# Two-layer adaLN block on one core: the chunk recurrence reordered, its widenings split between two engines, and bf16 filler products at TensorE's waits

## The reference

```python
def attn(q, k, v):
    s = einsum('bqhd,bkhd->bhqk', q, k) / sqrt(16)
    return einsum('bhqk,bkhd->bqhd', softmax(s), v)

def step(carry, xs):                         # 32 steps, one after the other
    W_in, W_out = carry
    q_t, k_t, v_t, lr_t = xs                 # 16 tokens
    k_h = softmax(einsum('blhd,bDhd->blhD', k_t, W_in)) * lr_t[..., 1:]
    q_h = softmax(einsum('blhd,bDhd->blhD', q_t, W_in))
    qk = einsum('bqhD,bkhD->bhqk', q_h, k_h) * mask
    o_t = einsum('bqhD,bDhd->bqhd', q_h, W_out) + einsum('bhqk,bkhd->bqhd', qk, v_t)
    W_out = W_out + einsum('bnhD,bnhd->bDhd', k_h, v_t)
    for _ in range(2):
        g_out = -attn(W_in, k_t, v_t)
        g_in = -attn(W_out, v_t, k_t)
        W_in = W_in - lr_in * g_in           # lr of the chunk's first token
        W_out = W_out - lr_out * g_out
    return (W_in, W_out), o_t
```

## Time and profile before

| | |
|---|---|
| time, three runs | median 3272.44 us (3271.39 to 3279.75) |
| the profiled execution | 3277.18 us, its span 3275.4 us |
| TensorE busy over the span | 2825.2 us, 86% |
| VectorE, ScalarE, GpSimd | 53%, 46%, 28% |
| granted TensorE clock over the span | 0.826 of full speed |

### The profile page before, as it was taken

The page is one execution under the profiler, slowest core; times in us unless marked ns, Lnnn a source line. Parts: engine busy times, 40 slices in busy tenths (PEclk is TensorE's granted clock), DMA queues, the critical chain, the costliest instruction groups (busy, mean ns, idle before and its releaser), DMA issues.

```text
span 3275.4 us, 89426 instructions
## 1 busy us (share of the span) xinstructions
PE 2825.2 (86%) x33209; PEld 1802.3 (55%) x33209; DVE 1720.1 (53%) x3951; ACT 1512.3 (46%) x3677; POOL 903.8 (28%) x1029
## 2 busy tenths in 40 slices
PE   6999947887888888788869999999989999999998
PEld 4444425655665656565535646556464664655556
DVE  3888834444444444444335546465564655646455
ACT  3878743233333323233225547364463635637355
POOL 0212113433333333333311313212132221323213
PEclk8999966655655565566579999999999999999999
DMA  5555571212131221211021010111101111011110
GB/s 159 154 157 163 160 158 39 55 29 56 36 68 36 50 60 29 56 36 29 9 77 39 17 56 22 52 39 53 38 15 40 39 53 39 15 44 36 53 39 14
DMA packets 386706, 189.99 MB, mean 58 GB/s; under 512 B 271664, under 2 KB 371632, under 8 KB 386224
## 3 DMA queue, kind: packets, MB, share of 16 engines
q1 hardware_dynamic: 386256, 184.01, 22.0%
HBM read 90.10 MB, written 71.30 MB: 49 GB/s over the span
## 4 chain that ended last, share of the span: by engine, by line
PE 64%; DVE 13%; ACT 9%; issue 9%; POOL 1%; DMA 1%; SPq 1%; DVEq 0%; ACTq 0%; POOLq 0%
PE psum L948 8%; PE psum L797 6%; PE psum L793 6%; PE psum L781 5%; PE psum L788 5%; PE psum L710 5%; PE psum L1029 3%; DVE arena L1592 3%; PE psum L1063 3%; PE psum L1052 3%; PE psum L987 2%; DVE arena L1659 2%; ACT arena L1385 2%; PE psum L1081 2%; PE psum L995 2%
## 5 line engine op out<-in xcount | busy, mean ns | idle before, releaser
L1233 ACT ACTIVATE arena<-psum,scan_sb 128x128 f32<-128x128 f32 x768 | 210.8, 408 | 305.4 <-PE psum L891 198.9
L1527 POOL TENSOR_TENSOR arena<-arena 128x400 f32<-128x400 f32 x256 | 218.8, 855 | 473.5 <-DVE arena L1929 473.5
L1445 POOL TENSOR_TENSOR arena<-arena 128x512 f32<-128x512 f32 x132 | 139.8, 1059 | 722.7 <-ACT arena L1250 708.5
L1659 DVE TENSOR_TENSOR arena<-psum,scan_sb 128x512 f32<-128x512 f32 x386 | 245.8, 685 | 175.1 <-PE psum L879 102.4
L1385 ACT ACTIVATE arena<-psum,arena 128x100 f32<-128x100 f32 x1024 | 268.0, 346 | 127.6 <-DVE arena L1921 127.6
L797 PEld LDWEIGHTS psum<-arena,scan_sb 32*128 32x128 f32 x1056 | 196.3, 274 | 170.2 <-issue 170.2
L793 PE MATMUL psum<-arena,scan_sb 128*128 128x512 f32 x264 | 230.7, 971 | 24.5 <-ACT arena L1239 24.4
L788 PE MATMUL psum<-arena 128*32 128x17 f32 x10240 | 197.0, 207 | 57.1 <-DVE arena L1659 22.2
L1592 DVE SCALAR_TENSOR_TENSOR arena<-psum,taps_sb,arena 128x511 f32<-128x511 f32 (+2 forms) x288 | 213.8, 747 | 61.0 <-ACT arena L1144 54.2
L781 PE MATMUL psum<-arena 128*32 128x32 f32 (+1 forms) x8192 | 190.9, 219 | 60.7 <-DVE arena L1659 43.9
L1921 DVE TENSOR_REDUCE arena<-psum 128x4 f32<-128x400 f32 x256 | 147.2, 575 | 179.0 <-PE psum L1052 177.6
(11 more groups left out here) (215 smaller groups left out, 5099.4 us busy)
## 6 DMA issues: line engine op xcount, KB each, us to landing
arena<-arena SPq DMA_DIRECT2D x144, 128.0 KB
arena<-x SPq DMA_DIRECT2D x32, 512.0 KB, 4.1
arena<-o_d SPq DMA_DIRECT2D x18, 512.0 KB, 5.8
arena<-gate_d SPq DMA_DIRECT2D x18, 512.0 KB, 6.6
v_rows_d<-arena SPq DMA_DIRECT2D x64, 136.0 KB
k_rows_d<-arena SPq DMA_DIRECT2D x64, 136.0 KB
arena<-k_rows_d SPq DMA_DIRECT2D x128, 68.0 KB, 2.1
arena<-v_rows_d SPq DMA_DIRECT2D x128, 68.0 KB, 2.1
```

The costliest lines, as they stand in the source:

```text
L1527: pool.tensor_tensor(soft, soft, c_rec[s].unsqueeze(2).broadcast_to([P, 4, KEYS]), ALU.mult).then_inc(c_pool.mark(f"prob{s}{f}"), 1)
L1659: return dve.tensor_tensor(dst.rearrange("p (t x a) -> p t x a", x=PP, a=INNER)[:, tiles], src.rearrange("p (t a) -> p t a", a=INNER)[:, t ...
```

## The change

On TensorE, `running` is taken apart into `sums(j)` and `add_state(js)`, which adds the state for two j at once with j as the inner loop. Halves of widenings disappear: every `scores` and `updates` walks over all four strips. `p1v` and `p2v` come ahead of `khv`, and `two`, `tw1` and `b0`, `b1` stand in pairs. `keep_busy` (new) issues 19 filler products a chunk into a bank that nobody reads. The two states' `ti1` and `ti` change places. On the other engines, each of now 8 widenings is done by two engines at once: VectorE writes partitions 0 to 63 and four copies in one instruction, ScalarE partitions 64 to 127 and the four others in four instructions. What neither writes stays zero from one memset of 9216 columns ahead of the loop. In the diff the first `spread` is ScalarE's, the second VectorE's. Stages A and C, the loads and GpSimd's steps are as before, though GpSimd and ScalarE wait for `r01` or `r23` where they waited for one `r`.

```diff
+            def keep_busy(count):
+                for _ in range(count):
+                    pe.matmul(bank[5][:, 0:2 * KT * KEYS], identb[:], mask_sb[:, 0:2].rearrange("p a b -> p (a b)"), start=True, stop=True)
...
-            def running(j, w_out):
-                mm = pe.matmul(bank[6 + j % 2][:], causal, kv[:, j], start=True, stop=False, skip_group_check=True)
-                rows = slice(j * NST, (j + 1) * NST)
+            def sums(j):
+                return pe.matmul(bank[6 + j % 2][:], causal, kv[:, j], start=True, stop=False, skip_group_check=True)
+
+            def add_state(js, w_out):
                 for a in range(INNER):
-                    dst = bank[6 + j % 2][:].rearrange("q (p a d) -> q p a d", p=PP, a=INNER)[:, :, a]
-                    mm = pe.matmul(dst, pick_row[rows, a], w_out[rows].rearrange("q (p d) -> q p d", p=PP),
-                                   start=False, stop=(a == INNER - 1), skip_group_check=True)
+                    for j in js:
+                        rows = slice(j * NST, (j + 1) * NST)
+                        dst = bank[6 + j % 2][:].rearrange("q (p a d) -> q p a d", p=PP, a=INNER)[:, :, a]
+                        mm = pe.matmul(dst, pick_row[rows, a], w_out[rows].rearrange("q (p d) -> q p d", p=PP),
+                                       start=False, stop=(a == INNER - 1), skip_group_check=True)
...
+                    keep_busy(4)
+                    pe.wait_ge(dve.sem, dve.before(c, "xi"))
                     pe.wait_ge(act.sem, act.before(c, "xi"))
-                    pe.wait_ge(dve.sem, dve.before(c, "xb11"))
...
+                    pe.wait_ge(dve.sem, dve.at(c, "x1"))
+                    pe.wait_ge(act.sem, act.at(c, "x1"))
+                    updates(grid(bank[0][:, 0:PP * ROW17], ROW17), pb_1, v_rows[i % 2], every).then_inc(mine.mark("p1v"), 1)
...
             def spread(dst, src):
-                for x in range(PP):
-                    ins = act.activation(dst.rearrange("p (t x a) -> p t x a", x=PP, a=INNER)[:, :, x],
-                                         src.rearrange("p (t a) -> p t a", a=INNER), ACT.Copy, scale=mask8[:, x:x + 1])
+                for x in range(PP // 2, PP):
+                    ins = act.activation(dst.rearrange("p (t x a) -> p t x a", x=PP, a=INNER)[upper, :, x],
+                                         src.rearrange("p (t a) -> p t a", a=INNER)[upper], ACT.Copy, scale=mask8[upper, x:x + 1])
...
-            dve.memset(st_in1, 0.0).then_inc(st_dve.mark("no_st"), 1)
+            dve.memset(arena[:, 0:9 * TILES * NST], 0.0).then_inc(st_dve.mark("no_st"), 1)
...
-            def spread(dst, src, h):
-                tiles = slice(h * TILES // 2, (h + 1) * TILES // 2)
-                shape = [P, TILES // 2, PP, INNER]
+            def spread(dst, src, h=0):
+                rows, xs = slice(h * P // 2, (h + 1) * P // 2), slice(h * PP // 2, (h + 1) * PP // 2)
+                shape = [P // 2, TILES, PP // 2, INNER]
...
-                    dve.wait_ge(pe.sem, pe.at(c, "pb1"))
-                    dve.reciprocal(i_inv, i_new[:, :, :, HD]).then_inc(mine.mark("irec"), 1)
...
+                    for r, (before, after, name) in enumerate(((w_in_now, w_in_1, "wi1"), (w_in_1, w_in_now, "wi"))):
+                        dve.wait_ge(pe.sem, pe.at(c, f"pb{r}"))
+                        dve.reciprocal(i_inv[r], i_new[r][:, :, HD]).then_inc(mine.mark(f"irec{r}"), 1)
...
+                    dve.wait_ge(pe.sem, pe.at(c, "ti1"))
+                    spread(st_in1, bank[2][:, 0:P]).then_inc(mine.mark("xs"), 1)
                     dve.wait_ge(pe.sem, pe.at(c, "ti"))
-                    for h in range(2):
-                        spread(st_in2, bank[3][:, 3 * P:4 * P], h).then_inc(mine.mark(f"xi{h}"), 1)
+                    spread(st_in2, bank[1][:, 0:P]).then_inc(mine.mark("xi"), 1)
```

283 lines of the change are left out of this document (141 added, 142 removed).

## The result

The changed kernel takes 2909.8 us in the median of four runs (2907.7 to 2923.4), 0.889 of the kernel before (95% interval 0.886 to 0.892). The forecast was 2841 with a range of 2780 to 2965: the time lies in the range, 69 us above the forecast. The profiled execution has a span of 2907.3 us.

A forecast was written before the change was run, and what follows sets the result against it. TensorE's queue at the low clock was taken to bound a 35.75 us chunk. 21.0 + 0.5 + 0.2 + 0.8 = 22.5 us a chunk, 431 us less in all, gives 2846, less 4.7 for the median: 2841 us, range 2780 to 2965.

The forecast's parts named there:

- The bound before: Recurrence of the kernel before: a chunk of 35.75 us was said to be bound by TensorE's queue at the low clock.
- The path after: Changed chunk: VectorE leads `kmax` to `wok`, 8.0 us, TensorE's sums and state products beside it; TensorE waits for VectorE behind updates.
- The walk: Dependent chain of one changed chunk at full clock, from `a0` to the next, hand-offs priced from the rows: 21.0 us.
- The clock: Recurrence: nine tenths of it at full clock, the tenth at round starts and until it rises again, 0.8 us a chunk.
- the first rival: The wait before `two` lowers the clock in every chunk, half the recurrence is low: 26.0 us a chunk, 2953 us; chance 0.11.
- Blocks over four strips: Scores and updates over all four strips: 0.9 us a block at low clock, 0.56 at full, 0.7 with its tail.
- a widening: Shared between two engines side by side: 0.66 us on VectorE, 1.2 us on ScalarE.
- the group of state products: State products of two j alternating on TensorE: line 807's 16 records in 1.2 us at full clock.
- The rivals with dear widenings: ScalarE's four instructions take as long as eight, 2937 us, chance 0.07; widenings at 5 us make it slower, 3328 us, 0.04.
- What follows the last chunk: Outputs behind the last chunk, 24 us at the low clock, give 7 us; the last chunk itself gives 13.
- The step that failed: TensorE's products waiting for nothing that shows: 0.5 us a chunk at full clock, bounds 0 and 2, plus 0.2 for rounds' starts.
- The loads: Rows of the next chunk, behind the block load, land by about 22 us, needed at `p1v` about 27 us after; nothing added.

The follow-up runs named there:

- the fastest kernel: Changed kernel with block loads spread over four chunks, sums of output 1 between `p1v` and `p2v`, state products between `p2v` and `khv`: 2883.5 us, 0.879 of the kernel before.

## Why the forecast was 69 us low

- **The bound before.** TensorE's queue at 1.2 GHz held the old kernel. Fillers alone, which make this queue longer and its clock faster, gave 5.2%: right.
- **The path after.** The walk let VectorE lead from `kmax` to `wok` for 8.0 us, with TensorE's sums and state products beside it, and had TensorE wait for VectorE behind the updates. In the quiet chunk of the two windows `kmax` to the end of `wok` takes 8.1 us, but VectorE waits for the updates in it (1741 is `prec`, 1747 `xrec`, 1757 `wok`):

```profile
DVE arena L1757 <- PE psum L794: 21.6, 16, 3.1
...
DVE psum L1741 <- PE psum L794: 19.1, 30, 1.3
DVE psum L1747 <- PE psum L794: 9.6, 7, 1.5
```

  That is 1.6 us a chunk between 490 and 1240 us. So TensorE holds part of this stretch, and VectorE's own steps are shorter than in the walk. That the sum still fits is in part luck.
- **The clock.** Nine tenths of the recurrence at full clock were foreseen; 0.93 granted is 0.86 of the time. A lapse in every chunk, the first rival, would have shown one behind `khv` or `pb1`; 11 of the 12 quiet chunks have none. Fillers hold the clock from 0.77 to 0.93, but that is worth only 39 us here.
- **The walk.** 21.0 against 20.4 by the fit. Blocks over four strips take 0.73 us with their tail (0.7), a widening 0.67 and 1.08 to 1.13 (0.66 and 1.2), the group of state products 1.16 (1.2), the memset 7.7 and nothing on the path (8.2). The rivals with dear widenings fall with these rows. What follows the last chunk, and that chunk itself, gave 20.7 us (20).
- **The step that failed** is the 0.5 us of waits for nothing shown, with 0 and 2 as bounds, plus 0.2 for round starts. It measured 3.4 us. The 2.0 us by which a chunk is longer than forecast, 62 us in 31 chunks, are this term, 2.6 us of it by the fit, less the 0.6 by which the walk was long. Some 5 of the other 7 us are the 4.7 that I took off for a median below the profiled execution; here the two are 0.7 us apart. I had taken it from a kernel whose records ran at half the rate and in shorter rows, and argued that slack in TensorE's first half would cover it. The slack is not where the stalls are: they fall where a piece of 256 instructions ends, most often in rows of products, and the chain waits for those.
- **The loads.** "The cover here is thin, 5 us every fourth chunk" looked for rows that land late. They never did; the block loads cost time another way, by some 2 to 3 us of longer stalls in the chunk in which they run.

## What to carry over

A filler buys back time at the low clock. Price it anew after the order has changed, which may have bought most of that already, and count its instructions, since cut in four the same columns cost 42 us. When short products move next to each other and the clock doubles, ask how fast their instructions can come: look for a row of records that breaks off with a wait for nothing shown, and put a long product between the blocks. If the breaks lie a fixed number of records apart, whatever stands there, it is the supply of instructions and not a wait of the program. Take such a term from the stage with the highest rate of records, not from the slow one.

## What I had not expected of the hardware

**Instructions as a supply.** At 2.4 GHz TensorE ran through 138 records of short products (69 products) and as many of their weight loads in 1.7 us and then stood for 1.2 us, until 1.5 us after a 16 KB packet of instructions had landed. All 53 long stalls of the recurrence ended 1.2 to 1.7 us after such a packet. The Trainium skill, "Runtime: NRT & Kernel Launch", section "Instruction fetch mechanics", has refills in blocks of 16 KiB or 256 instructions, which the packets and the distances of 256 records confirm, but calls the cost of crossing one mostly hidden and prefers full unrolling. Here it isn't hidden (3.4 us a chunk of 24.5), and writing the rounds out gave no gain (2921 against 2910 us).

**VectorE held up by GpSimd.** `asub` took 0.291 to 0.293 us in all 32 chunks before, and I used this as a sign that nothing disturbs it. It was no sign: in that kernel no instruction of GpSimd ran beside any of the 32. In the changed kernel it takes up to 1.21 us, 0.60 in the mean. VectorE's `asub` (1714) and GpSimd's products (1504) in the second chunk:

```profile
510.22 1.21 DVE L1714 TENSOR_TENSOR arena<-arena 128x128 f32<-128x128 f32 x1
```
```profile
510.22 2.14 POOL L1504 TENSOR_TENSOR arena<-arena 128x512 f32<-128x512 f32 x2
```

Where one of these products runs when `asub` starts, `asub` ends about 0.15 us after it; where `asub` is first, it keeps 0.29 and GpSimd's product takes 1.21 instead of 1.06. That is the rule of the Trainium skill, "SBUF — State Buffer", section "Who interferes with whom": an instruction of VectorE with two inputs in SBUF and one of GpSimd that reads SBUF exclude each other. The trace agrees. It lengthens `asub`, a step of the chain, by 0.3 us a chunk, and by 0.5 in the fastest kernel (0.81 in the mean). Whether moving GpSimd's products would bring this back wasn't tried.
